# Start of a conditioned transformer block: weight loads in steps, setup rows on other engines, another order of TensorE's first passes

## The reference

```
rms(x)  = x * rsqrt(mean(x*x) + 1e-6)
y       = (t @ gamma.T) * rms(x) + (t @ beta.T)
q, k, v = y @ Wq.T, y @ Wk.T, y @ Wv.T             # 16 heads of 16
x2      = x + (t @ alpha.T) * (softmax(0.25 * q k^T) v @ Wo.T)
z       = (t @ gamma_f.T) * rms(x2) + (t @ beta_f.T)
x3      = x2 + (t @ alpha_f.T) * (silu(z @ gate.T) * (z @ hidden.T) @ out.T + out_b)
result  = (layernorm(x3) * w + b + tanh(t @ lin.T + lin_b)) * w + b
```

## Time and profile before

| | |
|---|---|
| median of 3 runs | 490.44 us (489.93 to 492.53) |
| the profiled execution | 493.41 us, its span 491.6 us |
| busy in the span | TensorE 97%, its weight loads 82%, VectorE 76%, GpSimd 56%, ScalarE 49% |
| mean granted TensorE clock | 0.983 of full |
| 40 slices of 12.3 us, granted clock in tenths | 9 9 5, then 9 in all but the last, 7 |
| chain that ended last | TensorE 89%, VectorE 3%, GpSimd, ScalarE and DMA 2% each |

### The profile page before, as it was taken

One profiled execution on the slowest core, in us unless ns is written; L12 is line 12 of the kernel. 1 busy time (PEld: TensorE's weight loads), 2 busy tenths in 40 slices (PEclk: granted clock), 3 DMA queues, 4 the chain that ended last, 5 costly groups with the idle time before them and its releaser, 6 DMA issues.

```text
span 491.6 us, 11925 instructions
## 1 busy us (share of the span) xinstructions
PE 474.5 (97%) x4547; PEld 402.7 (82%) x4547; DVE 373.2 (76%) x770; ACT 241.7 (49%) x373; POOL 273.4 (56%) x192
## 2 busy tenths in 40 slices
PE   7799999999999999999999999999999999999992
PEld 4677778898879987898888988798888988889992
DVE  5869776578877789777886788777896688774765
ACT  3765754246452655427462554536553375413341
POOL 3464655644577543855468445774538554626673
PEclk9959999999999999999999999999999999999997
DMA  8761086301822044500944027420645007400113
GB/s 198 249 169 48 1 212 150 54 2 40 219 71 83 1 141 116 139 10 0 230 65 110 0 76 180 107 43 0 171 97 138 0 11 162 127 4 1 44 47 82
DMA packets 36044, 44.23 MB, mean 90 GB/s; under 512 B 3120, under 2 KB 31024, under 8 KB 36016
## 3 DMA queue, kind: packets, MB, share of 16 engines
q1 hardware_dynamic: 36016, 43.85, 35.7%
HBM read 35.18 MB, written 4.47 MB: 81 GB/s over the span
## 4 chain that ended last, share of the span: by engine, by line
PE 89%; DVE 3%; POOL 2%; ACT 2%; DMA 2%; issue 1%; DVEq 0%; SPq 0%; POOLq 0%
PE banks L767 31%; PE banks L785 17%; PE banks L510 7%; PE banks L616 6%; PE banks L806 5%; PE banks L700 4%; PE banks L545 4%; PE banks L659 3%; PE banks L664 3%; PE banks L822 2%; PE banks L604 2%; PE banks L581 2%; DMA x2g<-woT_in 2%; PE banks L467 1%; PE banks L737 1%
## 5 line engine op out<-in xcount | busy, mean ns | idle before, releaser
L767 PE MATMUL banks<-x2s,gh 128*128 128x512 f32 x672 | 167.5, 397 | 0.7 <-ACT x2s L1088 0.5
L767 PEld LDWEIGHTS banks<-x2s,gh 128*128 128x128 f32 x672 | 122.7, 188 | 28.1 <-issue 0.9
L1787 POOL TENSOR_TENSOR hs<-act_t,hs 128x512 fp32r<-128x512 f32 x56 | 72.0, 1286 | 126.5 <-ACT hs L1050 99.8
L785 PE MATMUL banks<-wout,hs 128*128 128x256 f32 x672 | 91.6, 285 | 0.5 <-POOL hs L1787 0.5
L785 PEld LDWEIGHTS banks<-wout,hs 128*128 128x128 f32 x672 | 85.3, 188 | 5.3 <-POOL hs L1787 0.7
L1050 ACT ACTIVATE hs<-act_t 128x512 fp32r<-128x512 f32 x56 | 35.3, 630 | 70.7 <-DVE act_t L1461 70.6
L1043 ACT ACTIVATE act_t<-banks 128x512 f32<-128x512 f32 x56 | 33.5, 598 | 68.7 <-PE banks L767 68.2
L1457 DVE SCALAR_TENSOR_TENSOR act_t<-act_t,banks 128x512 f32<-128x512 f32 x56 | 38.4, 685 | 31.2 <-ACT act_t L1043 30.8
L1371 DVE RECIPROCAL work_c<-banks 128x512 f32<-128x512 f32 x14 | 47.0, 3355 | 3.3 <-PE banks L659 3.3
L510 PE MATMUL banks<-xs,wqk 128*128 128x512 f32 x192 | 47.6, 394 | 0.7 <-ACT xs L978 0.7
L1461 DVE SCALAR_TENSOR_TENSOR act_t<-act_t,banks 128x512 f32<-128x512 f32 x56 | 38.5, 687 | 5.1 <-PE banks L767 2.0
(11 more groups left out here) (158 smaller groups left out, 748.9 us busy)
## 6 DMA issues: line engine op xcount, KB each, us to landing
xtok<-x_in SPq DMA_DIRECT2D x8, 512.0 KB, 5.1
work_c<-xn SPq DMA_DIRECT2D x16, 256.0 KB, 3.5
row_aa<-rows_dram SPq DMA_DIRECT2D x16, 256.0 KB, 6.9
xres<-x_in SPq DMA_DIRECT2D x8, 512.0 KB, 7.2
row_af<-rows_dram SPq DMA_DIRECT2D x16, 256.0 KB, 7.4
row_b<-rows_dram SPq DMA_DIRECT2D x16, 256.0 KB, 6.1
shift<-rows_dram SPq DMA_DIRECT2D x16, 256.0 KB, 6.0
y<-final SPq DMA_DIRECT2D x7, 512.0 KB, 3.2
```

The costliest lines, as they stand in the source:

```text
L767: last = mm(banks[:, base + part, :], gh[:, a, k, w:w + P], x2s[:, b, k, :], start=(n == 0), stop=(n == 5))
L785: last = mm(banks[:, t // 2, D * (t % 2):D * (t % 2) + D], hs[:, c % 2, b, P * t:P * t + P], wout[:, a, c, :], start=(c == 0 and a == b an ...
L1787: tt(hs[:, c % 2, 1, :], act_t[:, c % 2, :], hs[:, c % 2, 0, :].bitcast(F32), ALU.subtract)\
```

## The change

- SyncE waits for chunk 2 to land before it issues chunks 3 and 4, and for chunk 3 before 5 and 6. The rows' store waits for the new semaphores of the rows.
- ScalarE makes the selectors at the start of its list; the rows that VectorE took out of the banks are copied by ScalarE (`copy_rows`); K's first two forms come ahead of chunk 2's cut; the tanh comes after V is placed.
- VectorE loses its setup rows. GpSimd gets them (`join_rows`) after the scaling of the second x, and finishes the shift row after chunk 4.
- TensorE projects V's tiles 0 and 1 before island one, tiles 2 and 3 after it; waits for all four forms of K and transposes the second x ahead of island four; the counts are now WARM_LAST_MAX = 4, WARM_MAX = 7, WARM_NORM = 1; in `head(1)` the transposes of x2 stand ahead of the whole projection of Q.

```diff
--- before.py
+++ after.py
@@ -50,10 +50,10 @@
 ROOT_STEPS = 1 + 4 + 3
 LD_TABLE = 16 * 3
 LD_SHIFT = 16 * 4
-SETUP_TANH, SETUP_ALPHAS, SETUP_SHIFT = 1, 4, 3
-
-
-WARM_LOADS, WARM_LAST_MAX, WARM_MAX, WARM_NORM = 3, 2, 2, 3
+SETUP_COPIES, SETUP_SHIFT = 3, 3
+
+
+WARM_LOADS, WARM_LAST_MAX, WARM_MAX, WARM_NORM = 3, 4, 7, 1
 BLOCKS = 2 * CH
 LAG = 3
 V_EARLY = 3
@@ -170,8 +170,8 @@
         ld_stage = [sem("ld_stage%d" % n) for n in range(9)]
         out_stored, rows_stored, rs_stored = map(sem, ("out_stored", "rows_stored", "rs_stored"))
         zeroed, selectors_ready = sem("zeroed"), sem("selectors_ready")
-        tables_mm, rows_mm, tables_ready, identb_ready, setup_dve, setup_act, setup_pool = map(
-            sem, ("tables_mm", "rows_mm", "tables_ready", "identb_ready", "setup_dve", "setup_act", "setup_pool"))
+        tables_mm, rows_mm, tables_ready, identb_ready, rows_copied, rows_joined, setup_act, setup_pool = map(
+            sem, ("tables_mm", "rows_mm", "tables_ready", "identb_ready", "rows_copied", "rows_joined", "setup_act", "setup_pool"))
         stage_hi, stage_lo = sem("stage_hi"), sem("stage_lo")
         k_mm, q_mm, v_mm, s_mm, mt_mm, st_mm, den_mm, o_mm, xt_mm, op_mm, x2t_mm, gate_mm, hidden_mm, out_mm = map(
             sem, ("k_mm", "q_mm", "v_mm", "s_mm", "mt_mm", "st_mm", "den_mm", "o_mm", "xt_mm", "op_mm", "x2t_mm",
@@ -395,11 +395,14 @@
                 sp.dma_start(dst, src.to_broadcast([P, D])).then_inc(ld_lin, 16)
             load_x(1)
             load_stage(2)
+            sp.wait_ge(ld_stage[2], 16)
             load_stage(3)
             load_stage(4)
+            sp.wait_ge(ld_stage[3], 16)
             load_stage(5)
             load_stage(6)
-            sp.wait_ge(setup_dve, SETUP_ALPHAS)
+            sp.wait_ge(rows_copied, SETUP_COPIES)
+            sp.wait_ge(rows_joined, 2)
             sp.dma_start(rows_dram[:, 0:R_SHIFT, :], rows[:, 0:R_SHIFT, :]).then_inc(rows_stored, 16)
             move_v(0)
             sp.wait_ge(rows_stored, 16)
@@ -524,7 +527,8 @@
                 if rowed(g):
                     pe.wait_ge(k_ready, 4 * g + 4)
                 elif not later(g):
-                    pe.wait_ge(tables_ready, 3)
+                    pe.wait_ge(tables_ready, 2)
+                    pe.wait_ge(rows_copied, SETUP_COPIES)
                 project_qk(g, 0, bank_of_q(g), q_mm)
 
             def v_proj(g):
@@ -537,14 +541,18 @@
                     pe.wait_ge(h_steps, 2 * CH * (g - 1))
                 else:
                     pe.wait_ge(x2_steps, X2)
-                project_v(base, range(V_EARLY if later(g) else TT))
-
-            def project_v(base, tiles):
+                if later(g):
+                    project_v(base, range(V_EARLY), v_mm)
+                else:
+                    project_v(base, range(2))
+
+            def project_v(base, tiles, done=None):
                 for t in tiles:
                     for n, (k, a, b) in enumerate(passes):
                         last = mm(banks[:, base + t // 2, D * (t % 2):D * (t % 2) + D],
                                   xs[:, a, k, P * t:P * t + P], wv[:, b, k, :], start=(n == 0), stop=(n == 5))
-                last.then_inc(v_mm, 1)
+                if done is not None:
+                    last.then_inc(done, 1)
 
             def v_rest(g):
 
@@ -552,7 +560,7 @@
                     pe.wait_ge(x3_steps, X3 * (g - 1))
                 else:
                     pe.wait_ge(v_out, 2)
-                project_v(-(V_EARLY // 2), range(V_EARLY, TT))
+                project_v(-(V_EARLY // 2), range(V_EARLY, TT), v_mm)
 
             def scores_for_max(g, n):
 
@@ -835,9 +843,8 @@
                     ffn_out(g - 2, CH - 1)
                     q_proj(g)
                 else:
-                    project_qk(g, 0, bank_of_q(g), q_mm, (0,))
                     transpose_x2(g - 1)
-                    project_qk(g, 0, bank_of_q(g), q_mm, (1,))
+                    q_proj(g)
                     pe.wait_ge(k_ready, 4 * g + 4)
                     warm_up(wqk[:, 0, 0], WARM_NORM, bank_of_k(g))
 
@@ -847,12 +854,14 @@
                 q_proj(0)
                 v_proj(0)
                 scores_for_max(0, 0)
+                project_v(bank_of_v(0), (2, 3), v_mm)
                 scores_for_max(0, 1)
                 scores_for_max(0, 2)
                 pe.wait_ge(v_out, 1)
                 warm_up(wqk[:, 0, 0], WARM_LAST_MAX, 7)
+                pe.wait_ge(k_ready, 4)
+                transpose_x(1)
                 scores_for_max(0, 3)
-                transpose_x(1)
                 warm_up(wqk[:, 0, 0], WARM_MAX, 7)
                 pe.wait_ge(max_ready, 4)
                 pe.wait_ge(identb_ready, 2)
@@ -966,6 +975,20 @@
                 act.wait_ge(ld_stage[n], 16)
                 nc.scalar.activation(chunks[n][1], stage_view(n), ACT.Copy).then_inc(stage_hi, 1)
 
+            def setup_selectors():
+                act.wait_ge(ld_tables, LD_TABLE)
+                nc.scalar.activation(sel[:, :, :].rearrange("p c (e k) -> p (c e) k", e=2),
+                                     cst[:, C_SEL:C_SEL + 2 * G * SEQ].unsqueeze(2).to_broadcast([P, 2 * G * SEQ, L]),
+                                     ACT.Copy).then_inc(selectors_ready, 1)
+
+            def copy_rows():
+                act.wait_ge(rows_mm, 1)
+                nc.scalar.activation(cvec, banks[0:B, 2, 0:D], ACT.Copy).then_inc(rows_copied, 1)
+                nc.scalar.activation(rows[:, R_AA, :], banks[0:B, 2, D:2 * D], ACT.Copy).then_inc(rows_copied, 1)
+                act.wait_ge(tables_ready, 2)
+                nc.scalar.activation(rows[:, R_AF, :], banks[0:B, TABLE_BANK[OTHER_TABLES], D:2 * D], ACT.Copy)\
+                    .then_inc(rows_copied, 1)
+
             def setup_identity():
                 act.wait_ge(ld_tables, LD_TABLE)
                 for e in range(2):
@@ -1117,23 +1140,22 @@
                 pair_q(g)
 
             def first():
+                setup_selectors()
                 cut_hi(0)
                 cut_hi(1)
                 setup_identity()
                 x0_split()
-                nc.scalar.activation(sel[:, :, :].rearrange("p c (e k) -> p (c e) k", e=2),
-                                     cst[:, C_SEL:C_SEL + 2 * G * SEQ].unsqueeze(2).to_broadcast([P, 2 * G * SEQ, L]),
-                                     ACT.Copy).then_inc(selectors_ready, 1)
-                act.wait_ge(setup_dve, SETUP_TANH)
-                nc.scalar.activation(cvec, cvec, ACT.Tanh).then_inc(setup_act, 1)
+                copy_rows()
+                pair_k(0, range(2))
                 cut_hi(2)
-                pair_k(0, range(2))
                 cut_hi(3)
                 pair_q(0)
                 keep_v(0)
                 par_k(0)
                 act.wait_ge(zeroed, ZEROED)
                 place_v_kept(0)
+                act.wait_ge(rows_joined, 1)
+                nc.scalar.activation(cvec, cvec, ACT.Tanh).then_inc(setup_act, 1)
                 cut_hi(4)
                 place_v_swapped(0)
                 first_exp(0)
@@ -1271,19 +1293,6 @@
                 dve.wait_ge(tables_mm, n)
                 V.tensor_copy(tabs[:, TABLE_SLOT[names]:TABLE_SLOT[names] + len(names)].rearrange("p t k b -> p (t k b)"),
                               banks[:, TABLE_BANK[names], 0:len(names) * KD * B]).then_inc(tables_ready, 1)
-                if names == OTHER_TABLES:
-                    V.tensor_copy(rows[:, R_AF, :], banks[0:B, TABLE_BANK[names], D:2 * D]).then_inc(tables_ready, 1)
-
-            def setup_rows():
-                dve.wait_ge(ld_lin, LD_SHIFT)
-                dve.wait_ge(rows_mm, 1)
-                V.tensor_tensor(cvec, banks[0:B, 2, 0:D], linb_b[0:B], ALU.add).then_inc(setup_dve, 1)
-                V.tensor_copy(rows[:, R_AA, :], banks[0:B, 2, D:2 * D]).then_inc(setup_dve, 1)
-
-            def setup_weights():
-                V.tensor_tensor(w2[:, :], lnw_b, lnw_b, ALU.mult).then_inc(setup_dve, 1)
-                dve.wait_ge(tables_ready, 3)
-                V.tensor_tensor(rows[:, R_B, :], rows[:, R_AF, :], outb_b[0:B], ALU.mult).then_inc(setup_dve, 1)
 
             def square_sum(x, scratch, total, done):
                 V.tensor_tensor_reduce(out=scratch, in0=x, in1=x, scale=1.0, scalar=0.0, op0=ALU.mult, op1=ALU.add,
@@ -1550,8 +1559,6 @@
                 q_out(g)
 
             def first():
-                setup_rows()
-                setup_weights()
                 dve.wait_ge(stage_lo, 1)
                 stats_x(1, x2n)
                 dve.wait_ge(x_stats, XS * 2)
@@ -1762,6 +1769,14 @@
                 pool.wait_ge(x2_steps, X2 * f + X2)
                 tt(x2c[:, :, :], x2[:, :, :], row_b[:, :, :], ALU.add).then_inc(x2_kept, 1)
 
+            def join_rows():
+
+                pool.wait_ge(ld_lin, LD_SHIFT)
+                pool.wait_ge(rows_copied, SETUP_COPIES)
+                tt(cvec, cvec, linb_b[0:B], ALU.add).then_inc(rows_joined, 1)
```

(6 more changed lines are left out.)

## The result

The changed kernel takes 492.52 us in the median of 12 executions (491.23 to 494.09), the kernel before 490.34 (12 executions on the same chip); the ratio is 1.004, with a 95% interval of 1.0025 to 1.0055. So it is about 2 us slower. That lies inside the range of the prediction and inside its "within 0.5%", but the forecast was no change, and the interval excludes that.

A forecast was written before the change was run, and what follows sets the result against it. It took TensorE's waits and low clock in the start as the bound; -3.0 + 0.9 + 0.9 - 0.3 = -1.5, with 1.5 put back for the median: 490.44 - 1.5 + 1.5 = 490.4 us, range 487.4 to 494.0.

The forecast's parts named there:

- the clock term: TensorE's start, group 0: clock stays high, 3.0 us gained in an execution like the profiled one; median assumed to have half.
- rival 3: Start: the change does nothing for the clock because the median had none of the fall; 491.9 us, chance 0.1.
- The steps: SyncE's waits between weight loads: first gate chunk lands at 21.4, Q written 0.9 us later; nothing for W_o and x.
- rival 2: Load queue: SyncE's waits free it, x and W_o 1.2 us earlier, Q 0.3 early, clock high; 487.7 us, chance 0.21.
- Order and passes: TensorE's first list: island four behind K's forms and transposes, then seven passes; costs 0.9 us at the high clock.
- rival 1: TensorE's start: the clock falls anyway and the added passes run at the low level; 493.3 us, chance 0.21.
- Setup rows and ScalarE's order: Setup on ScalarE, VectorE, GpSimd: moved rows cost 0; K written 2 us earlier, lost waiting for the first gate chunk.
- The head: Head of group 1: transposes of x2 no longer behind six Q passes, GpSimd's beta earlier; gain 0.3 us.
- The step on VectorE: VectorE's setup: five operations of about 0.4 us and one copy leave, but it waited for x, so gains nothing.

The follow-up runs named there:

- the ordinary execution of before: Profile of the kernel before with one wait more on SyncE, for a load that landed long ago; 491.07 us in the median, ratio to before 1.0005.
- changed again: The changed kernel run once more, unaltered, on the same chip as its variants; 493.62 us, ratio to before 1.0045.
- rest: Changed kernel without load waits, TensorE's first list and passes as before, six waits more on VectorE; 490.38 us, ratio to before 0.9977.
- the pad: Six waits more on VectorE, on a semaphore long reached; on the changed kernel 492.46 us, ratio to before 1.0022.

## Why the prediction was wrong

- **The step that failed is the clock term.** The prediction read 3.0 us from one profiled execution and took it that "the median had half of the 3.0 already", so that 1.5 us was left to gain. There was none: four in five executions of before don't have the long low stretch, and the median clock is 0.989 or 0.990 in every set of before and 0.990 after. With the 1.5 put back the sum gives 491.9, the prediction's own rival 3, which had a chance of 0.1. The evidence lay open: the profiled execution stood 3.0 us above the median, just the size of the term. The measured 492.5 is another 0.6 above that, and the terms below have room for it. The stated range held the time because it was wide, not because the forecast's mechanism was right.
- **The steps** were priced right in kind and about in size: 0.9 us for a chunk landing 3.4 us after its issue. It was 3.8 to 4.0 (the upper bound was 4.1), ScalarE waited for it, and on before it measures 1.4 us. It gave them nothing for x and W_o; there it was wrong: over all profiles both land about 1 us earlier with the steps, the premise of rival 2. In the profile after the chunk landed at 20.0 and Q was written from 21.03, 0.4 us ahead of the profile before, much as rival 2 had it (20.2, 0.3 early); but it is 0.5 us behind the ordinary execution of before (20.53).
- **Order and passes**: 0.9 forecast for a clock that stays high. Measured on before 0.5 in time and 0.7 in the stage; 0.3 to 1.4 in the stage at the high clock in all, by when K's last form is written, and 1.6 where the short low stretch lies over the transposes. That is rival 1's mechanism at 3.4 us of low clock, which the prediction priced for the long stretch alone.
- **Setup rows and ScalarE's order** were put at 0, since the wait for the chunk ate K's 2 us. Without the steps they are worth about 1 us, the head included; with the steps they were not measured alone. (The trace counts five VectorE operations less, 765 against 770, and not five and a copy.)
- **The head**: 0.3 forecast, seen in GpSimd's rows, too small to be told in the times.
- **What no step named** is the end: 0.8 us from VectorE's shorter list. The step on VectorE ("Five operations of about 0.4 us leave VectorE, and one copy", "so it gains nothing") looked at the stage they left and not at where its code is fetched 470 us later. Nor did it name the time outside the span, 0.25 to 0.5 us in the mean.

By ratios, from "changed again" one step at a time: without the fetch 1.1 us less, without the steps 0.5, without the order 1.7, and what is left stands 1.1 below before. That these add up to the 2.2 is no proof: differences taken in a row always do. Each is the difference of two ratios with intervals of some 0.9 us either way, the third over two chips. The parts taken by themselves are the test: steps 1.4, order 0.5 and head 0 on before, the end 0.8 in the traces, and rest -1.1 make 1.6 of the 2.2. What is missing is within the errors; the time outside the span is hardly in these parts.

## What to carry to other kernels

Hold the profiled execution against the other runs before a stall is read as the kernel's: where it stands above the median by just the size of the stall, the stall may well be that execution's, and the clocks of the single executions tell. A fix for such a stall puts its work or its wait on every execution, and here that cost more than it gave back. And where a change only removes instructions, look at the end of the span too: compare the time from the last store's issue to the end in both profiles.

## What the hardware did that was not expected

- With six VectorE instructions less, 470 us ahead of the end, and the rest of the change, one 8 KB fetch of code starts 1.0 us behind the last store's issue instead of 2.7 ahead of it; three more on VectorE alone put it 0.8 ahead again. Behind, it goes with a last landing 0.8 us later. That the fetch is VectorE's is shown by the pad, not by a name in the trace; that one engine of 16 is the late one is worked out from the trickle.
- With four and seven passes in TensorE's new order, 44 of 82 executions take 1.9 to 3.3 us beyond their span, and none of 196 does without them. No run shows why.
- The kernel before has 10.2 us of low clock in its start in both of its profiles, and 3.4 in the one with one idle wait more on SyncE; the mean clocks of its executions, 0.982 to 0.995, say that it has both, and in its fastest perhaps none. Its second x is summed from 17.4, 17.1 or, with that idle wait, 16.5 us.
